# Cross attention of a decoder layer: the weighted rest keys of a head group issued behind its eighth scores instead of between the sixth and the seventh

## The reference

```python
x = x + attn(layernorm(x), w_q, w_k, w_v, w_o)            # causal, 16 heads of 64
x = x + xattn(layernorm(x), ctx, ctx, ...)                # differential cross attention
x = x + ffn(layernorm(x), w1, conv_w, conv_b, w2)         # quantised, depthwise convolution
# xattn: 16 heads of 8, each in two halves of 4
logits_1 = q1 @ k1.T * SCALING ; logits_2 = q2 @ k2.T * SCALING
diff_weights = softmax(logits_1) - lam * softmax(logits_2)
output = ((diff_weights @ v) * (1 - LAMBDA_INIT)) @ out_proj_weight.T + out_proj_bias
```

## Time and profile before

| | |
|---|---|
| median of 3 executions | 298.13 us (297.63 to 299.05) |
| the profiled execution | 297.73 us, span 295.6 us |
| TensorE busy | 279.4 us, 95% |
| VectorE busy | 214.6 us, 73% |
| ScalarE busy | 194.4 us, 66% |
| granted TensorE clock | 1.00 |

### The profile page before, as it was taken

The page is one execution under the profiler, slowest core; times in us unless marked ns, Lnnn a source line. Parts: engine busy times, 40 slices in busy tenths (PEclk is TensorE's granted clock), DMA queues, the critical chain, the costliest instruction groups (busy, mean ns, idle before and its releaser), DMA issues.

```text
span 295.6 us, 6630 instructions
## 1 busy us (share of the span) xinstructions
PE 279.4 (95%) x2442; PEld 177.5 (60%) x2442; DVE 214.6 (73%) x481; ACT 194.4 (66%) x485; POOL 147.5 (50%) x267
## 2 busy tenths in 40 slices
PE   0899999999999999999999999899999998999996
PEld 0567666666666659666666677445445553357674
DVE  3678778878776670877776756987988769645865
ACT  2587587777777770677777930677777676844754
POOL 3706957885477793298565500069127282100162
PEclk9999999999999999999999999999999999999999
DMA  7930000000000000000000000000000001000001
GB/s 272 294 141 3 0 3 1 2 2 0 3 2 3 0 2 2 0 3 0 3 2 2 2 2 0 2 0 0 2 0 1 2 1 39 0 0 2 0 18 53
DMA packets 4978, 6.42 MB, mean 22 GB/s; under 512 B 850, under 2 KB 3666, under 8 KB 4820
## 3 DMA queue, kind: packets, MB, share of 16 engines
q1 hardware_dynamic: 4372, 5.55, 5.5%
q10 hardware_dynamic: 576, 0.47, 0.5%
HBM read 5.49 MB, written 0.52 MB: 20 GB/s over the span
## 4 chain that ended last, share of the span: by engine, by line
PE 75%; DVE 11%; POOL 5%; ACT 5%; issue 2%; DMA 1%; DVEq 0%; ACTq 0%
PE bank L760 65%; PE bank L831 7%; DVE qk L1486 3%; POOL pr L340 2%; DVE stats L1358 1%; POOL cw_sb L417 1%; POOL qk L423 1%; PE bank L983 1%; DVE nmax L1441 1%; DMA x_sb<-in_x 1%; ACT pr L566 1%; POOL pT L340 1%; PE bank L885 1%; DVE xn L1374 1%; DVE mv L1363 1%
## 5 line engine op out<-in xcount | busy, mean ns | idle before, releaser
L665 ACT ACTIVATE pT<-bank 128x512 f32<-128x512 f32 (+1 forms) x80 | 44.5, 601 | 25.6 <-PE bank L760 25.3
L566 ACT ACTIVATE pr<-bank,nmax 128x256 f32<-128x256 f32 (+2 forms) x96 | 44.3, 480 | 22.9 <-DVE nmax L1441 22.7
L1486 DVE TENSOR_REDUCE qk<-bank 128x4 fp32r<-128x616 f32 x64 | 49.1, 796 | 13.5 <-PE bank L760 13.4
L340 POOL TENSOR_SCALAR pr<-pr,pinv 128x256 f32<-128x256 f32 (+2 forms) x96 | 45.5, 490 | 23.8 <-DVE pinv L1449 23.6
L760 PE MATMUL bank<-qs 64*128 64x256 f32 (+3 forms) x256 | 49.5, 470 | 0.3 <-ACT qs L545 0.3
L1441 DVE TENSOR_REDUCE nmax<-bank 128x2 f32<-128x512 f32 (+2 forms) x48 | 31.7, 688 | 11.4 <-PE bank L760 11.3
L760 PE MATMUL bank<-pT,v_sb 128*64 128x128 f32 (+2 forms) x320 | 38.6, 385 | 0.0
L340 POOL TENSOR_SCALAR pT<-pT,pinv 128x512 f32<-128x512 f32 x32 | 22.0, 699 | 23.1 <-DVE pinv L1449 23.1
L1457 DVE COPY pT<-bank 128x512 f32<-128x512 f32 (+1 forms) x32 | 30.4, 949 | 1.4 <-PE bank L831 1.4
L760 PEld LDWEIGHTS bank<-pT,v_sb 128*64 128x64 f32 x320 | 21.0, 136 | 13.9 <-issue 10.6
L760 PE MATMUL bank<-km,qk 64*128 64x308 f32 x128 | 27.7, 366 | 1.2 <-DVE qk L1486 1.1
(11 more groups left out here) (193 smaller groups left out, 570.9 us busy)
## 6 DMA issues: line engine op xcount, KB each, us to landing
pT<-in_wqk SPq DMA_DIRECT2D x1, 1024.0 KB, 6.1
cw_sb<-in_cw SPq DMA_DIRECT2D x1, 768.0 KB, 8.5
x_sb<-in_x SPq DMA_DIRECT2D x2, 256.0 KB, 5.3
pT<-in_wv SPq DMA_DIRECT2D x1, 512.0 KB, 6.9
wo_sb<-in_wo SPq DMA_DIRECT2D x1, 512.0 KB, 7.1
out<-x_sb SPq DMA_DIRECT2D x6, 64.0 KB, 1.5
onT<-in_consts ACTq DMA_DIRECT2D x1, 256.0 KB, 6.3
pT<-in_xwk SPq DMA_DIRECT2D x1, 256.0 KB, 7.4
```

Of the source, the lines that this page charges most:

```text
L340: nc.gpsimd.tensor_scalar(d, d, pinv[:, t, a:a + 1], 1.0, ALU.mult, ALU.mult).then_inc(norm_done, 1)
L566: nc.scalar.activation(prob[r][:, a, at:at + w], bank[:, SP[k % 2] + a, at:at + w], ACT.Exp, bias=nmax[:, t, a:a + 1], accum_out=psum[:, t ...
L665: nc.scalar.activation(px[rows, i, :], bank[rows, (ST0, ST1)[i % 2], :], ACT.Exp, scale=SD ** -0.5).then_inc(xexp_done, 1)
L1486: nc.vector.tensor_reduce(m, s_in, AX.X, ALU.max, negate=True).then_inc(round_done, 1)
```

## The change

`cross_weighted_rest(G)` is called later in the loop over groups, behind the eighth scores and directly ahead of `turn_cross_max`, or of the second `turn_sums(1, 1)` in the last group. Nothing else is edited.

```diff
@@ -1277,7 +1277,6 @@
                     next_max(G, 4)
                     reduced = rounds[0]
                 cross_scores(G, 5)
-                cross_weighted_rest(G)
                 cross_scores(G, 6)
                 if more:
                     next_max(G, 5)
@@ -1291,6 +1290,7 @@
                     part_sums = rounds[0]
                     turn_sums(1, 0)
                 cross_scores(G, 7)
+                cross_weighted_rest(G)
                 if more:
                     turn_cross_max(G + 1, reduced)
                 else:
```

## The result

The changed kernel takes **315.11 us** (median of 4, 310.13 to 318.61) against 298.59 us before: the ratio is 1.0473, interval 1.0433 to 1.0513. The ratio is that of the two executions near the fastest (310.13 and 314.41 us); over the medians of all it is 315.11 / 298.59 = 1.055. Forecast were 302.2 us, 300.3 to 303.8. The sign was right, the size was not: by the medians 16.5 us were lost where 4.3 were forecast.

A forecast was written before the change was run, and what follows sets the result against it. It took TensorE, busy 48.99 of 50.00 us at clock 1.00, as the bound. Each group adds 1.00 us less what the seventh scores come forward, with waits counted: +4.3 us in all, forecast 302.2 us, range 300.3 to 303.8.

The forecast's parts named there:

- The sum of the shifts: Groups 0 to 7 of the cross attention: 0 + 0.41 + 0.88 + 0.53 + 0.49 + 0.53 + 0.53 + 0.90 = +4.3 us.
- the idle row of group 0: TensorE's 0.36 us wait for VectorE before 194.43 us swallows group 0's shift; forecast still there at the same time.
- the unknowns that it lists: Follower's wait 0 or 0.2 us in three groups, group 0 perhaps 0.3, swallowed part 0.6 to 2: total 2.2 to 5.6.
- the case of the drains: Rival: each group saves a change of tile shape, 0.18 us, eight times 1.4, giving 296.7 us; chance 0.04.
- the step of 0.25 us: In the drains rival: time from a score to the next of the same shape, against 0.32 to another shape.
- nothing changes: Rival: ScalarE's or VectorE's list sets the pace of the groups and the shift is slack, 298.1 us; chance 0.05.
- half is swallowed: Rival: waits for VectorE swallow some 2 of the 4.3 us, giving 300.3 us; chance 0.13.
- The whole-block case: Rival: seventh scores come no sooner, so all groups pay the whole block, 8 x 1.00, 306.1 us; chance 0.03.

The follow-up runs named there:

- the half filler: Changed kernel plus the rest keys' four matmuls also issued over 256 of 512 columns at the old place in each group: 302.67 us, ratio 1.0137.

## Why the prediction was right and wrong

**The step that failed** is in its first paragraph: the clock of 1.00 was read off the rows of before and kept for the changed kernel, and so "every pause between two of its blocks, counts one for one". A pause costs its length and, when the clock falls behind it, about 0.4 us for each microsecond at the lower level: 12.4 of the 16.5 us. The forecast named the pauses, with their places and lengths, and never asked what they would do to the clock; no rival did either, and the range ended at 303.8. What the runs showed in its place is a clock that depends on the pauses: 0.939 to 0.972 with them, 1.00 in every execution with half a block in them.

**The sum of the shifts was right.** 4.3 us forecast; with the clock held at 1.00 measured 4.1 by the times and 4.5 by the trace. In parts: groups 1, 3, 4, 5 together 2.0, measured 1.8 in one execution and 2.2 in the trace of another; group 6 0.53, measured 0.5 (1.0016, with an interval that holds zero); group 2 0.88, 299.13 as the middle of the five at full clock, against 298.08, so 1.0; group 0 nothing, measured nothing once the clock was held (0.9997); group 7 0.90, measured 0.75 in the trace of the half filler. The one execution with only group 7 late that stayed at full clock, 300.25 us, is 2.2 above its comparison; the shift doesn't explain that.

**What it foresaw in the profile**: idle time in front of the seventh scores, 0.29 us in group 4 and 0.87 and 0.98 in groups 2 and 7 (forecast 0.3 to 0.6, and near 1); sixth to seventh scores in group 4 242.37 - 241.68 = 0.69 us (forecast 0.75). **What it got wrong there**: that TensorE's busy time would stay (it went from 279.4 to 292.4 us), and that the idle row of group 0 would stay at its place. That row is gone even where the clock was held (group 0 late and filled): a wait that swallows a shift gets shorter by it, so the forecast contradicted itself here.

**Sums that don't come out**: the unknowns that it lists reach up to 4.3 + 0.24 + 0.3 = 4.8 us, not 5.6, and down to 4.3 - 0.36 - 2 = 1.9, not 2.2. In the case of the drains the step of 0.25 us is 0.26 in the earlier trace rows and lies behind a maximum's scores of 308 columns, which is no like step. The measured time lies far outside either way.

**The rivals.** That the drains decide, or that nothing changes, fell with the sign; that half is swallowed (300.3 us) fell with the half filler's 302.7. The whole-block case gave 306.1 us, nearer than the forecast, but that would be luck: its reason isn't there, since only groups 2 and 7 paid for most of the block.

**What stays open** is which pauses bring the clock down. Group 0's, 0.20 us with three others of 0.17 to 0.40 us in the 5.3 us ahead of it, came with the lower clock in all four executions; group 6's, 0.69 us behind one of 0.60, in one of ten; group 2's in half; group 7's in nine of ten. In the kernel with groups 1, 3, 4, 5 and 6 the profiled execution fell behind group 6, and the other three have the same mean clock of 0.989. The same program at the same places falls or doesn't, so something that differs between executions has a part in it. The runs show that filling the pauses keeps the clock, not a length from which one is dangerous. The kernel before is close to it as well: 3 of its 45 executions in the comparisons show a clock of 0.982 and 301.9 to 303.2 us.

None of the kernels beats the one before. Its rest keys do two jobs at the old place, their own and covering the time in which the exponentials free a score bank.

## What to carry to other kernels

Work that waits for nothing is worth most where TensorE would otherwise wait for another engine; before moving it, work out the pause that it leaves (here the seventh scores start 0.05 us behind the end of the fifth exponentials). On a kernel like this one, with TensorE busy 95% of the span, price a new pause twice: its length, and the chance that the granted clock falls behind it, which here made the loss four times as large (16.5 us for 4.1). When a moved block costs far more than the shifts explain, look at the row of the granted clock first, and test it by filling the pause with waste: a kernel that does more and gets faster has named its cause.

## What the runs showed of the hardware

No pause of TensorE ahead of the falls shown here was longer than 0.98 us, and in the stretches ahead of two of them it was still busy 12.81 of 14.00 us and 5.82 of 6.80 us. Even so the granted clock dropped from 2.4 to 1.2 GHz, for 3.4 to 14 us, and stayed there while TensorE worked without a break (10.90 of 10.90 us busy at 0.50). The Trainium skill, "TensorE: Matmul & The Clock Gate", A second HAM failure mode, describes a kernel in which TensorE "micro-idles between MM groups frequently enough" for its clock to swing between these two levels; this case's traces agree, with falls behind pauses of 0.20 to 0.98 us. In the four executions of the changed kernel the clock was 0.972, 0.956, 0.944 and 0.939 for 310.1, 314.4, 315.8 and 318.6 us: the spread of one program's times is that of its clock.
